# The reciprocals of the key features' sums: one VectorE instruction per batch becomes four GpSimd instructions

## The chip, the cores and the metric

The kernel runs on one core of a Trainium2 chip. The time is device microseconds of one execution of the whole program. "Before" is the median of three runs, and a further execution was profiled. TensorE multiplies matrices into the PSUM memory, VectorE (DVE in the rows) and ScalarE (ACT) compute on SBUF and PSUM, GpSimd (POOL) computes on SBUF alone, and SyncE (SP) issues DMAs. Each engine runs its own list of instructions in order and waits on semaphores that the others raise.

## The reference, cut to what matters

There are 32 batches of 256 tokens with 128 channels, in 16 heads of 8. Each batch is normalised and projected to q, k and v. The output mixes a sparse attention (the 12 largest scores of each row) with a linear one, on softmax features of q and k:

```python
q = _layernorm(q, q_gamma, q_beta)
k = _layernorm(k, k_gamma, k_beta)
scores = jnp.einsum('bhnd,bhmd->bhnm', q, k) / jnp.sqrt(jnp.float32(D))
aw = jax.nn.softmax(scores, axis=-1)
kth = jax.lax.top_k(aw, topk)[0][..., -1:]
...
kf = jax.nn.softmax(k, axis=-1)
kv = jnp.einsum('bhnd,bhne->bhde', kf, v)
```

The change concerns `kf`: the exponentials of a key's 8 values are divided by their sum. With 256 tokens on 128 partitions and 16 heads, that makes 32 sums on each partition and batch.

## The kernel before, in words

Every engine walks the same loop: iterations `it` from -2 to 33, and in each eight units `u_` of two heads. A unit holds four score tiles of 128x256. Iteration `it` works on batch `it`'s scores and prepares batch `it + 1`; its last units serve the batches on both sides. The order on each engine is the written order of its block.

One unit passes through the engines like this:

- TensorE makes the scores (L907). VectorE takes the 8 largest of each row from the four tiles (`largest`, `top`, L613).
- GpSimd subtracts the maximum (`drop`, L402), and ScalarE makes the exponentials of the four tiles (`e`, L803) and of the 8 largest (`e8`, L808).
- One unit later VectorE removes the 8 largest from `e` (`remove`, L620, which waits for `e8`) and takes the next 8 (`following`, `next8`, L626). Between these stand small steps for the other stages (`extra`).
- One more unit later GpSimd and ScalarE share the comparisons (`below`). GpSimd makes `POOL_TILES` = 3, 2, 3, 4, 4, 4, 3, 2 of the four tiles for the eight units (L424), in its own units 2 to 7, 0 and 1. TensorE then transposes, and so on.

On GpSimd, `drop` of a unit stands ahead of the unit's other work, and so behind all of the unit before it.

The key features of batch `it + 1`: ScalarE makes `k_exp` (L844); GpSimd adds the 8 values in three steps in unit 5 (`k_half`, `k_quarter`, `k_sum`, L453); VectorE takes the reciprocal in unit 6 (`k_rec`, L685), ahead of its last `following`; GpSimd multiplies in unit 7 (`k_feat`, L460).

Ahead of batch 0 stands a prologue. There VectorE passes the reciprocal of batch 0 in iteration -1, and then runs `stage_gate` (L585 to L602), which chooses one of eight feed-forward matrices, ahead of its first `top`.

Of the kernel before, what the change touches and what calls it, by code (L numbers as in the profile page):

```python
# [26 lines left out]
ALU = mybir.AluOpType  # L27
# [3 lines left out]
P = 128  # L31
H = 16
# [3 lines left out]
NT = N // P  # L36
# [48 lines left out]
def build(nc, x, Wqkv, bqkv, q_gamma, q_beta, k_gamma, k_beta, alpha, Wproj, bproj, W, bW, logits, u, y):  # L85
# [12 lines left out]
    def exists(batch):  # L98
        return not isinstance(batch, int) or 0 <= batch < B

    with ExitStack() as ctx:
        def sb(name, shape, dt=F32):
            return ctx.enter_context(nc.sbuf_tensor(name, shape, dt))
# [4 lines left out]
        def sem(name):  # L108
            return ctx.enter_context(nc.semaphore(name))
# [60 lines left out]
        k_half = sb("k_half", [P, NT * H, 4])  # L170
        k_quarter = sb("k_quarter", [P, NT * H, 2])
        k_sum = sb("k_sum", [P, NT * H])
        k_rec = sb("k_rec", [P, NT * H])
        k_feat = sb("k_feat", [P, NT, C])
        v_aug = sb("v_aug", [P, 2, NT, H, VW])
# [34 lines left out]
            x_stats x_mean x_rsqrt_step x_rsqrt_ready x_newton xn_ready  # L210
            w_xT xT_copied w_qk_ready sq_ready sq_step raw_ready ss_ready qk_rsqrt_step qk_rsqrt_ready qk_newton
            n_step qkn_ready w_qkT w_rest part_ready slots_written first_loaded slots_loaded
            dmax_ready dsub_ready dexp_ready ksum_step ksum_ready krec_ready feat_ready
            w_v_ready v_copied w_kv kv_ready w_qfT qfT_copied w_lin linz_step lin_ready
            w_turn den_step osp_ready w_osT osT_copied w_out y_ready""".split()
        s = {n: sem(n) for n in names}
# [68 lines left out]
        def _(pool):  # L285
            def select(out, op, fill, base_, pattern, mult, n):
                pool.wait_ge(s["pool_step"], n)
                return nc.gpsimd.affine_select(out=out, in_=out, compare_op=op, fill=fill, base=base_,
                                               pattern=pattern, channel_multiplier=mult)
# [11 lines left out]
            for par in range(2):  # L301
                nc.gpsimd.memset(v_aug[:, par, :, :, D:VA], 1.0).then_inc(s["pool_const"], 1)
            nc.gpsimd.memset(top[:], 0.0).then_inc(s["pool_const"], 1)
            nc.gpsimd.memset(eps_row[:], 0.0).then_inc(s["pool_step"], 1)
            pool.wait_ge(s["pool_step"], 6)
            nc.gpsimd.memset(eps_row[:, :, D:VA], Z_EPS).then_inc(s["pool_const"], 1)
# [5 lines left out]
            select(used, ALU.not_equal, 1.0, 0, [[-VW, 4], [-1, VA]], 1, 7).then_inc(s["gather_ready"], 1)  # L312
            select(spare, ALU.not_equal, 1.0, -VA, [[-VW, 4], [-1, VW - VA]], 1, 7).then_inc(s["gather_ready"], 1)
            select(minus_one[:], ALU.not_equal, -1.0, 0, [[-1, P]], 1, 8).then_inc(s["gather_ready"], 1)
            pool.wait_ge(s["pool_const"], 7)
            gb = gamma[:].rearrange("p a h d -> p (a h d)")
            bb = beta[:].rearrange("p a h d -> p (a h d)")

# [72 lines left out]
            def body(it, par, xr):  # L391
                nxt = 1 - par
                for u_ in range(UNITS):
                    if (it, u_) == (-2, 7):
                        stage_shares()
                    g = it * UNITS + u_
                    if exists(it):

                        q = u_ % 2
                        wait(pool, s["e8_ready"], g - 1)  # L400
                        wait_alone(pool, s["top_ready"], TILES * (g + 1), s["waits_passed"])
                        nc.gpsimd.tensor_tensor(drop[:, q], top[:, q], top[:, q, :, 1:2].to_broadcast(  # L402
                            [P, TILES, 9]), ALU.subtract).then_inc(s["drop_ready"], 1)
                    if u_ == 0 and it >= 0 and exists(it + 1):

                        pool.wait_ge(s["sq_ready"], it + 2)
                        src = qk_sq[:].rearrange("p (g d) -> p g d", d=D)
                        for i, (dst, w) in enumerate(((sq_half[:], 4), (sq_quarter[:], 2),
                                                      (qk_ss[:].unsqueeze(2), 1))):
                            if i:  # L410
                                pool.wait_ge(s["sq_step"], 2 * it + i)
                            nc.gpsimd.tensor_tensor(dst, src[:, :, 0:w], src[:, :, w:2 * w], ALU.add).then_inc(
                                s["sq_step" if i < 2 else "ss_ready"], 1)
                            src = dst
                    if u_ == 2 and it >= 0 and exists(it + 1):
                        normalise(it, 1)
                    if u_ == 3 and it >= 0 and exists(it + 1):
                        normalise(it, 2)
                    if exists(it if u_ >= 2 else it - 1):

                        r = (u_ - 2) % RING
                        for t in range(POOL_TILES[r]):
                            wait_alone(pool, s["next_ready"], TILES * (g - 2) + t + 1, s["waits_passed"])
                            nc.gpsimd.tensor_scalar(below[:, r, t, :], e[:, r, t, :],  # L424
                                                    next8[:, r, t, TOPK - 9:TOPK - 8], None,
                                                    ALU.is_lt).then_inc(s["below_pool"], 1)
                    if u_ == 1 and it >= 0 and exists(it + 1):
                        normalise(it, 0)
                    if u_ == 3 and it >= 0 and exists(it + 1):

                        pool.wait_ge(s["dmax_ready"], it + 2)
                        nc.gpsimd.tensor_tensor(heads(d_sub[:]), heads(qkn[:]), spread(d_max[:]),
                                                ALU.subtract).then_inc(s["dsub_ready"], 1)
                    if u_ == 4 and it >= -1 and exists(it + 2):

                        pool.wait_ge(s["x_rsqrt_ready"], 2 * (it + 3))
                        n = X_STEPS * (it + 2)
                        refine(x_rsqrt, "x", n)
                        pool.wait_ge(s["x_newton"], n + 3)
                        nc.gpsimd.tensor_tensor(x_shift[:, 0], x_mv[:, :, 0], x_rsqrt[:, 3],  # L440
                                                ALU.mult).then_inc(s["x_newton"], 1)
                        wait_alone(pool, s["x_newton"], n + 4, s["waits_passed"])
                        nc.gpsimd.tensor_scalar(x_shift[:, 1], x_shift[:, 0], -1.0, None,
                                                ALU.mult).then_inc(s["x_newton"], 1)
                    if u_ == 5 and exists(it + 1):

                        pool.wait_ge(s["dexp_ready"], 2 * (it + 2))
                        src = k_exp[:].rearrange("p t (h d) -> p (t h) d", d=D)
                        for i, (dst, w) in enumerate(((k_half[:], 4), (k_quarter[:], 2),
                                                      (k_sum[:].unsqueeze(2), 1))):  # L450
                            if i:
                                pool.wait_ge(s["ksum_step"], 2 * (it + 1) + i)
                            nc.gpsimd.tensor_tensor(dst, src[:, :, 0:w], src[:, :, w:2 * w], ALU.add).then_inc(  # L453
                                s["ksum_step" if i < 2 else "ksum_ready"], 1)
                            src = dst
                    if u_ == 7 and exists(it + 1):

                        pool.wait_ge(s["krec_ready"], it + 2)
                        pool.wait_ge(s["dexp_ready"], 2 * (it + 2))
                        nc.gpsimd.tensor_tensor(k_feat[:].rearrange("p t (h d) -> p (t h) d", d=D),  # L460
                                                k_exp[:].rearrange("p t (h d) -> p (t h) d", d=D),
                                                k_rec[:].unsqueeze(2).to_broadcast([P, NT * H, D]),
                                                ALU.mult).then_inc(s["feat_ready"], 1)
# [4 lines left out]
        def _(dve):  # L468
# [73 lines left out]
            def stage_normalise():  # L542
# [34 lines left out]

                dve.wait_ge(s["bq_centred"], 1)
                in_parts(b_row[:, 0:2 * C], slice(0, 2 * C)).then_inc(s["bqk_ready"], 1)
                dve.wait_ge(s["pool_const"], 7)  # L580
                nc.vector.tensor_tensor(own_head[:, :, 0:D], own_head[:, :, 0:D],
                                        mix[:, 6, :].unsqueeze(2).to_broadcast([P, H, D]),
                                        ALU.mult).then_inc(s["head_ready"], 1)
# [23 lines left out]
            def body(it, par, xr):  # L607
# [20 lines left out]
                def extra(u_, k):  # L628
# [25 lines left out]
                    if u_ == 5 and 1 <= k <= 4 and exists(it - 1):  # L654
                        w = pv_ps[:, 0:NT * H * VA].rearrange("p (g e) -> p g e", e=VA)
                        n = 2 * (it - 1)
# [14 lines left out]
                    if u_ == 1 and exists(it + 2):  # L671
# [5 lines left out]
                        if k == 5:  # L677
# [2 lines left out]
                            alone(s["x_newton"], X_STEPS * (it + 2))  # L680
                            for t in range(NT):
                                nc.vector.bn_aggr(x_mv[:, t], stats[:, t]).then_inc(s["x_mean"], 1)  # L682
                    if u_ == 6 and exists(it + 1) and k == 5:
                        dve.wait_ge(s["ksum_ready"], it + 2)
                        nc.vector.reciprocal(k_rec[:], k_sum[:]).then_inc(s["krec_ready"], 1)  # L685

                for u_ in range(UNITS):
                    if (it, u_) == (-2, 2):
# [192 lines left out]
        def _(pe):  # L881
# [8 lines left out]
            def body(it, par, xr):  # L890
# [76 lines left out]
                def early(u_):  # L967
# [47 lines left out]
                    if u_ == 7 and exists(it + 2):  # L1015

                        pe.wait_ge(s["xT_copied"], it + 4)
                        if it == -2:
                            pe.wait_ge(s["wqk_ready"], 1)
                            pe.wait_ge(s["bq_centred"], 1)  # L1020
                            pe.wait_ge(s["pool_const"], 7)
                            pe.wait_ge(s["gather_ready"], 4)
                        if it == -1:
                            pe.wait_ge(s["bqk_ready"], 1)
# [93 lines left out]
```

## Time and profile before

| | |
|---|---|
| median of 3 runs (lowest to highest) | 1223.74 us (1223.39 to 1226.09) |
| the profiled execution | 1223.17 us |
| its span, first to last instruction | 1221.4 us |
| mean granted TensorE clock | 0.978 of full speed |
| VectorE busy | 1186.8 us, 97% of the span |
| ScalarE busy | 1086.6 us, 89% |
| GpSimd busy | 1081.7 us, 89% |
| TensorE busy | 959.2 us, 79% |

The 1.8 us between the profiled execution and its span lie outside of the first and the last instruction. Shares of busy time are averages over the span; idle time counts only where it delays the engine that ends last.

### The profile page before, as it was taken

To read this page: it belongs to the slowest core of one execution; us is meant where nothing else is said; L and a number is where in the kernel's file an instruction comes from. 1 tells how busy PE (TensorE), PEld (TensorE's weight loads), DVE (VectorE), ACT (ScalarE), POOL (GpSimd) and SP (SyncE) were. 2 spreads that over 40 slices of the span, in tenths; PEclk is the share of its full clock that TensorE was granted. 3 is DMA by queue.
4 is the path that set the end of the run, shared out by engine and by line. 5 is a ranking of instruction groups with operands and counts; after the bars stand their busy time and mean duration, and the time that the engine had idled before them with its cause. 6 is when DMAs were issued, how large, how long until landed. Compare 5 with 4: busy or idle time off the path is not lost.

```text
span 1221.4 us, 34664 instructions
## 1 busy us (share of the span) xinstructions
PE 959.2 (79%) x8999; PEld 651.6 (53%) x9030; DVE 1186.8 (97%) x4540; ACT 1086.6 (89%) x3626; POOL 1081.7 (89%) x1688
## 2 busy tenths in 40 slices
PE   4478878788887887887888877878787878887776
PEld 2255555555555555555555555555555555555554
DVE  5999999999999999999999999999999999999994
ACT  3589999999999999899999999999999999999984
POOL 5599999999999999999999999999999999999964
PEclk9999999999999999999989999999999999999998
DMA  3122221222221212221112222122222122222110
GB/s 94 30 62 79 84 83 40 69 60 83 84 83 50 62 57 84 84 84 55 56 58 84 83 84 60 55 67 70 84 83 80 40 62 70 83 84 79 45 45 14
DMA packets 165127, 82.78 MB, mean 68 GB/s; under 512 B 7737, under 2 KB 164927, under 8 KB 164930
## 3 DMA queue, kind: packets, MB, share of 16 engines
q1 hardware_dynamic: 164658, 80.43, 22.9%
q8 instruction: 74, 1.21, 0.4%
q14 instruction: 123, 1.01, 0.3%
q10 hardware_dynamic: 272, 0.13, 0.0%
HBM read 42.78 MB, written 37.75 MB: 66 GB/s over the span
## 4 chain that ended last, share of the span: by engine, by line
DVE 64%; issue 25%; DVEq 4%; PE 4%; ACT 2%; POOL 1%; DMA 0%; POOLq 0%; ACTq 0%
DVE rest L620 27%; DVE top L613 22%; DVE next L626 9%; DVEq L75 4%; DVE o_sparse L668 1%; DVE lin_z L641 1%; POOL below L424 1%; ACT e L803 1%; PE turn_ps L925 1%; DVE stats L676 0%; DVE den L660 0%; DVE kv L634 0%; PE work_ps L1027 0%; DVE x_mv L682 0%; PE pv_ps L946 0%
## 5 line engine op out<-in xcount | busy, mean ns | idle before, releaser
L424 POOL TENSOR_SCALAR below<-e,next 128x256 bf16<-128x256 f32 x800 | 724.3, 921 | 0.7 <-issue 0.6
L803 ACT ACTIVATE e<-score_ps,drop 128x256 f32<-128x256 f32 x1024 | 471.6, 478 | 67.5 <-POOL drop L402 63.9
L620 DVE MATCH_REPLACE8 rest<-e 128x256 f32<-128x256 f32 x1024 | 432.7, 431 | 0.0
L925 PE MATMUL turn_ps<-ident,e 128*128 128x128 f32 x2048 | 397.5, 288 | 39.6 <-ACT kept L773 18.3
L626 DVE MAX8 next<-rest 128x8 f32<-128x256 f32 x1024 | 427.7, 434 | 0.3 <-issue 0.2
L926 PE MATMUL turn_ps<-minus_huge,below 128*128 128x128 bf16 x2048 | 377.0, 224 | 0.0
L613 DVE MAX8 top<-score_ps 128x8 f32<-128x256 f32 x1024 | 365.5, 436 | 1.1 <-PE score_ps L907 1.1
L925 PEld LDWEIGHTS turn_ps<-ident,e 128*128 128x128 f32 x2048 | 295.5, 144 | 76.7 <-issue 32.5
L773 ACT ACTIVATE kept<-turn_ps 128x1024 f32<-128x1024 f32 x256 | 267.5, 1045 | 32.8 <-PE turn_ps L926 32.4
L926 PEld LDWEIGHTS turn_ps<-minus_huge,below 128*128 128x128 bf16 x2048 | 221.2, 108 | 0.7
L803 ACT ACTIVATION_READ_ACCUMULATOR e<-score_ps,drop 128x1 f32 x1024 | 214.9, 210 | 0.0
L946 PE MATMUL pv_ps<-kept,v_aug 128*32 128x256 f32 x2048 | 142.8, 398 | 1.9 <-ACT out_sb L849 1.3
L402 POOL TENSOR_TENSOR drop<-top 128x36 f32<-128x36 f32 x256 | 62.7, 245 | 64.4 <-DVE top L613 63.9
L907 PE MATMUL score_ps<-k_slots,q_slots 64*128 64x256 bf16 x1024 | 102.8, 278 | 20.8 <-issue 9.9
L816 ACT ACTIVATE below<-e,next 128x256 bf16<-128x256 f32 x224 | 107.7, 514 | 0.0
L620 DVE MATCH_VALUE_LOAD rest<-e 128x8 f32 x1024 | 97.7, 95 | 1.9 <-ACT e L808 1.9
L946 PEld LDWEIGHTS pv_ps<-kept,v_aug 128*32 128x32 f32 x2048 | 55.3, 112 | 48.8 <-issue 28.8
L907 PEld LDWEIGHTS score_ps<-k_slots,q_slots 64*128 64x128 bf16 x1024 | 30.7, 94 | 79.8 <-issue 72.4
L1027 PE MATMUL work_ps<-w_qk,xnT 128*128 128x256 f32 x128 | 46.8, 449 | 31.1 <-ACT xnT L865 31.1
L808 ACT ACTIVATE e<-drop 128x32 f32<-128x32 f32 x256 | 62.7, 245 | 0.0
L957 PE MATMUL pv_ps<-gather,oT 128*128 128x128 f32 x256 | 35.0, 280 | 33.1 <-ACT oT L825 33.1
L1049 PE MATMUL work_ps<-kv,qfT 128*128 128x144 f32 x128 | 25.1, 321 | 40.3 <-DVE kv L634 40.3
(182 smaller groups left out, 1341.1 us busy)
## 6 DMA issues: line engine op xcount, KB each, us to landing
part_slots<-part SPq DMA_DIRECT2D x128, 192.0 KB, 2.3
q_slots<-part_slots SPq DMA_DIRECT2D x64, 256.0 KB, 3.4
k_slots<-part_slots SPq DMA_DIRECT2D x64, 256.0 KB, 4.1
part_slots<-part SPq DMA_DIRECT2D x64, 128.0 KB, 1.9
x_sb<-in_L_attn_x SPq DMA_DIRECT2D x32, 128.0 KB, 4.0
x_res<-in_L_attn_x SPq DMA_DIRECT2D x32, 128.0 KB, 3.9
out_y<-out_sb SPq DMA_DIRECT2D x32, 128.0 KB, 4.1
w_ops<-in_L_ffn_W SPq DMA_DIRECT2D x1, 512.0 KB
```

The costliest lines, as they stand in the source:

```text
L402: nc.gpsimd.tensor_tensor(drop[:, q], top[:, q], top[:, q, :, 1:2].to_broadcast([P, TILES, 9]), ALU.subtract).then_inc(s["drop_ready"], 1)
L424: nc.gpsimd.tensor_scalar(below[:, r, t, :], e[:, r, t, :], next8[:, r, t, TOPK - 9:TOPK - 8], None, ALU.is_lt).then_inc(s["below_pool"], 1)
L613: nc.vector.max(top[:, q, t, 1:9], score_ps[:, q, t // 2, t % 2, :]).then_inc(s["top_ready"], 1)
L620: nc.vector.match_replace(rest[:, t, :], e8[:, (u_ - 1) % 2, t, :], e[:, (u_ - 1) % RING, t, :], REMOVED).then_inc(s["rest_ready"], 1)
L626: nc.vector.max(next8[:, (u_ - 1) % RING, t, :], rest[:, t, :]).then_inc(s["next_ready"], 1)
L773: nc.scalar.activation(kept[:, u_ % 4], turn_ps[:], ACT.Relu).then_inc(s["turn_copied"], 1)
L803: nc.scalar.activation(e[:, u_ % RING, t, :], score_ps[:, u_ % 2, t // 2, t % 2, :], ACT.Exp, bias=drop[:, u_ % 2, t, 0:1], accum_out=z[:, ...
L816: nc.scalar.activation(below[:, r, t, :], e[:, r, t, :], ACT.Relu, scale=-1.0, bias=next8[:, r, t, TOPK - 9:TOPK - 8]).then_inc(s["below_a ...
L907: last = mm(score_ps[:, v_ % 2, hh, nt, :], q_slots[rows, side, v_, nt * P:(nt + 1) * P], k_slots[rows, side, v_, :], start=True, stop=True)
L925: mm(dst, e[:, r, t, keys], ident[:], start=True, stop=False, is_transpose=True)
L926: last = mm(dst, below[:, r, t, keys], minus_huge[:], start=False, stop=True)
L946: last = mm(pv_ps[32 * j:32 * (j + 1), 0:N], v_aug[:, side, mc, 4 * q + j, :], kept[:, v_ % 4, j % 2, mc, :], start=(mc == 0), stop=(mc == ...
```

## The change

VectorE's reciprocal goes. GpSimd makes `k_rec` in unit 6, behind its comparisons of that unit: a power (`k_sum` to the -1, with the exponents read from a tile `inverse` that is filled once), and a Newton step on it in three instructions, each of which waits for the one before. The four stand ahead of unit 7's `drop`.

```diff
+        inverse = sb("inverse", [P, NT * H])
+        k_power = sb("k_power", [P, 2, NT * H])
...
+            nc.gpsimd.memset(inverse[:], -1.0).then_inc(s["pool_const"], 1)
...
-            pool.wait_ge(s["pool_const"], 7)
+            pool.wait_ge(s["pool_const"], 8)
...
+                    if u_ == 6 and exists(it + 1):
+
+                        first, near = k_power[:, 0], k_power[:, 1]
+                        n = 3 * (it + 1)
+                        pool.wait_ge(s["ksum_ready"], it + 2)
+                        nc.gpsimd.tensor_tensor(first, k_sum[:], inverse[:], ALU.pow).then_inc(s["krec_step"], 1)
+                        pool.wait_ge(s["krec_step"], n + 1)
+                        nc.gpsimd.tensor_tensor(near, first, k_sum[:], ALU.mult).then_inc(s["krec_step"], 1)
+                        pool.wait_ge(s["krec_step"], n + 2)
+                        nc.gpsimd.tensor_scalar(near, near, -1.0, 2.0, ALU.mult, ALU.add).then_inc(s["krec_step"], 1)
+                        pool.wait_ge(s["krec_step"], n + 3)
+                        nc.gpsimd.tensor_tensor(k_rec[:], first, near, ALU.mult).then_inc(s["krec_ready"], 1)
...
-                    if u_ == 6 and exists(it + 1) and k == 5:
-                        dve.wait_ge(s["ksum_ready"], it + 2)
-                        nc.vector.reciprocal(k_rec[:], k_sum[:]).then_inc(s["krec_ready"], 1)
```

VectorE's and TensorE's waits for `pool_const` go from 7 to 8 in the same way.

On GpSimd, units 5 to 7 of iteration 0 (preparing batch 1) read as follows before:

```order
L453 TENSOR_TENSOR k_sum<-k_quarter 128x32 [waits ksum_step]
L402 TENSOR_TENSOR drop<-top 128x36 [waits top_ready,e8_ready]
L424 TENSOR_SCALAR below<-e,next 128x256 [waits next_ready] x4
L402 TENSOR_TENSOR drop<-top 128x36 [waits top_ready,e8_ready]
L424 TENSOR_SCALAR below<-e,next 128x256 [waits next_ready] x4
L460 TENSOR_TENSOR k_feat<-k_exp,k_rec 128x256 [waits dexp_ready,krec_ready]
```

And with the change, from unit 6 on:

```order
L405 TENSOR_TENSOR drop<-top 128x36 [waits top_ready,e8_ready]
L427 TENSOR_SCALAR below<-e,next 128x256 [waits next_ready] x4
L464 TENSOR_TENSOR k_power<-k_sum,inverse 128x32 [waits ksum_ready]
L466 TENSOR_TENSOR k_power<-k_power,k_sum 128x32 [waits krec_step]
L468 TENSOR_SCALAR k_power<-k_power 128x32 [waits krec_step]
L470 TENSOR_TENSOR k_rec<-k_power 128x32 [waits krec_step]
L405 TENSOR_TENSOR drop<-top 128x36 [waits top_ready,e8_ready]
L427 TENSOR_SCALAR below<-e,next 128x256 [waits next_ready] x4
L475 TENSOR_TENSOR k_feat<-k_exp,k_rec 128x256 [waits dexp_ready,krec_ready]
```

The four new rows stand between unit 6's comparisons and unit 7's `drop`; nothing else moved there. The line numbers of the same instructions grow by 3 to 15.

In the prologue VectorE's rows around the reciprocal of batch 0 are these before (`bias` and `own_head` are the last steps of the stage ahead, the `gate` rows are the start of `stage_gate`):

```order
L489 SCALAR_TENSOR_TENSOR bias<-bias_rest,ident,bias_sum 3x256 [waits setup_p]
L581 TENSOR_TENSOR own_head<-own_head,mix 128x16x8 [waits pool_const]
L685 RECIPROCAL k_rec<-k_sum 128x32 [waits ksum_ready]
L587 TENSOR_SCALAR gate<-gate 128x8 [waits gate_logs]
L588 TENSOR_TENSOR gate<-gate 128x8 [waits setup_p]
```

And with the change:

```order
L504 SCALAR_TENSOR_TENSOR bias<-bias_rest,ident,bias_sum 3x256 [waits setup_p]
L596 TENSOR_TENSOR own_head<-own_head,mix 128x16x8 [waits pool_const]
L602 TENSOR_SCALAR gate<-gate 128x8 [waits gate_logs]
L603 TENSOR_TENSOR gate<-gate 128x8 [waits setup_p]
L604 TENSOR_REDUCE gate<-gate 128x1 [waits setup_p]
```

The reciprocal is gone, and with it VectorE's wait for `ksum_ready`: `stage_gate` follows at once.

## Rows read from the trace of the kernel before

**Rows 1.** The page's first part: busy us (share of the span) and instructions.

```profile
PE 959.2 (79%) x8999; PEld 651.6 (53%) x9030; DVE 1186.8 (97%) x4540; ACT 1086.6 (89%) x3626; POOL 1081.7 (89%) x1688
```

**Rows 2.** The chain that ended last, shares of the span by engine.

```profile
DVE 64%; issue 25%; DVEq 4%; PE 4%; ACT 2%; POOL 1%; DMA 0%; POOLq 0%; ACTq 0%
```

**Rows 3.** VectorE's timeline in a middle batch: start, duration in us.

```profile
647.18 1.42 DVE L613 MAX8 top<-score_ps 128x8 f32<-128x256 f32 x4
...
651.05 0.34 DVE L685 RECIPROCAL k_rec<-k_sum 128x32 f32<-128x32 f32 x1
...
651.59 1.41 DVE L613 MAX8 top<-score_ps 128x8 f32<-128x256 f32 x4
...
655.79 1.42 DVE L613 MAX8 top<-score_ps 128x8 f32<-128x256 f32 x4
657.12 0.08 DVE L620 MATCH_VALUE_LOAD rest<-e 128x8 f32 x1
...
666.04 0.08 DVE L620 MATCH_VALUE_LOAD rest<-e 128x8 f32 x1
```

**Rows 4.** Groups of VectorE's instructions: busy us, mean ns, idle before.

```profile
L685 DVE RECIPROCAL k_rec<-k_sum 128x32 f32<-128x32 f32 x32 | 11.4, 356 | 1.8 <-POOL k_sum L453 1.8
...
L660 DVE SCALAR_TENSOR_TENSOR den<-z,pv_ps 128x32 f32<-128x32 f32 x32 | 6.4, 200 | 11.2 <-PE pv_ps L957 11.2
```

**Rows 5.** VectorE's timeline in the prologue.

```profile
23.82 0.27 DVE L581 TENSOR_TENSOR own_head<-own_head,mix 128x128 f32<-128x128 f32 x1
25.89 0.35 DVE L685 RECIPROCAL k_rec<-k_sum 128x32 f32<-128x32 f32 x1 [1.80 <-POOL k_sum L453]
26.16 0.13 DVE L587 TENSOR_SCALAR gate<-gate 128x8 f32<-128x8 f32 x1
...
36.65 2.73 DVE L613 MAX8 top<-score_ps 128x8 f32<-128x256 f32 x8
```

**Rows 6.** TensorE's timeline in the prologue: the second unit's scores.

```profile
32.57 0.61 PE L907 MATMUL score_ps<-k_slots,q_slots 64*128 64x256 bf16 x4
```

**Rows 7.** GpSimd's timeline in the prologue: the first `drop`.

```profile
38.23 0.25 POOL L402 TENSOR_TENSOR drop<-top 128x36 f32<-128x36 f32 x1 [11.28 <-DVE top L613]
```

**Rows 8.** GpSimd's timeline in the middle batch; idle time before, and its releaser.

```profile
639.75 0.25 POOL L402 TENSOR_TENSOR drop<-top 128x36 f32<-128x36 f32 x1 [0.70 <-DVE top L613]
...
648.54 0.29 POOL L453 TENSOR_TENSOR k_quarter<-k_half 128x64 f32<-128x64 f32 x1
648.91 0.24 POOL L453 TENSOR_TENSOR k_sum<-k_quarter 128x32 f32<-128x32 f32 x1
...
653.21 0.24 POOL L402 TENSOR_TENSOR drop<-top 128x36 f32<-128x36 f32 x1 [0.27 <-DVE top L613]
...
670.77 0.24 POOL L402 TENSOR_TENSOR drop<-top 128x36 f32<-128x36 f32 x1 [0.26 <-DVE top L613]
...
674.32 1.08 POOL L432 TENSOR_TENSOR d_sub<-qkn,d_max 128x512 f32<-128x512 f32 x1 [0.28 <-DVE d_max L652]
```

**Rows 9.** GpSimd's waits over the span: us in total, times, longest.

```profile
POOL drop L402 <- DVE top L613: 63.9, 104, 11.3
POOL d_sub L432 <- DVE d_max L652: 8.3, 29, 0.3
```

**Rows 10.** Groups of GpSimd's instructions: busy us, mean ns, idle before.

```profile
L350 POOL TENSOR_TENSOR qk_b<-qk_a,gamma 128x512 f32<-128x512 f32 x31 | 39.5, 1273 | 0.0
...
L453 POOL TENSOR_TENSOR k_sum<-k_quarter 128x32 f32<-128x32 f32 x32 | 7.6, 238 | 2.5
...
L333 POOL TENSOR_SCALAR qk_rsqrt<-qk_rsqrt 128x64 f32<-128x64 f32 x31 | 7.5, 243 | 6.2 <-POOL qk_rsqrt L331 6.2
```

**Rows 11.** ScalarE's timeline in the middle batch.

```profile
653.49 0.47 ACT L803 ACTIVATE e<-score_ps,drop 128x256 f32<-128x256 f32 x1 [0.60 <-POOL drop L402]
...
655.30 0.24 ACT L808 ACTIVATE e<-drop 128x32 f32<-128x32 f32 x1
...
664.48 0.23 ACT L808 ACTIVATE e<-drop 128x32 f32<-128x32 f32 x1
```

More of the change, by code:

```diff
@@ L212, in build @@
             n_step qkn_ready w_qkT w_rest part_ready slots_written first_loaded slots_loaded
-            dmax_ready dsub_ready dexp_ready ksum_step ksum_ready krec_ready feat_ready
+            dmax_ready dsub_ready dexp_ready ksum_step ksum_ready krec_step krec_ready feat_ready
             w_v_ready v_copied w_kv kv_ready w_qfT qfT_copied w_lin linz_step lin_ready
@@ L579, in stage_normalise @@
                 in_parts(b_row[:, 0:2 * C], slice(0, 2 * C)).then_inc(s["bqk_ready"], 1)
-                dve.wait_ge(s["pool_const"], 7)
+                dve.wait_ge(s["pool_const"], 8)
                 nc.vector.tensor_tensor(own_head[:, :, 0:D], own_head[:, :, 0:D],
@@ L1020, in early @@
                             pe.wait_ge(s["bq_centred"], 1)
-                            pe.wait_ge(s["pool_const"], 7)
+                            pe.wait_ge(s["pool_const"], 8)
                             pe.wait_ge(s["gather_ready"], 4)
```

## The prediction, made before the changed kernel ran

> **What bounds the kernel now.** I read the busy times first: VectorE is busy for 1186.8 of 1221.4 us, the others for 89% or less [rows 1]. The chain that ended last says the same: 64% of it is VectorE's work and 25% "issue", time in which nothing that the profile shows was waited for [rows 2]. VectorE's timeline in a middle batch has no marked wait: from one `top` to the next a unit takes 4.41 us where the reciprocal stands in it (647.18 to 651.59) and 4.20 us in the next one (to 655.79) [rows 3]. So in the steady part every step that leaves VectorE's list shortens the batch, as long as no other engine becomes the bound.
>
> The next question is how far GpSimd is from that, since it takes the work. Its waits for VectorE in one batch are 0.27, 0.26 and 0.70 us ahead of three `drop`s and 0.28 us ahead of `d_sub` [rows 8]: **1.51 us** of real room a batch. Over the span it is (63.9 - 11.3 + 8.3) / 31 = 1.96 us a batch, with the prologue's one long wait taken out [rows 9]. That mean holds batches in which VectorE was itself held up, so I go by 1.51. GpSimd is thus nearly a second bound.
>
> **What is removed.** VectorE runs 32 reciprocals, 31 of them in the steady part and one in the prologue. Their profiled duration is 356 ns [rows 4], but instructions overlap on that engine, and what counts is the longer unit: 4.41 - 4.20 = 0.21 us [rows 3]. 31 x 0.21 = **6.5 us**. The upper bound is the full duration, 31 x 0.356 = 11.0 us; the difference of the units is the nearer reading, as it holds the overlap.
>
> The one in the prologue is worth more. `own_head` begins at 23.82 and ends at 24.09; VectorE then waits 1.80 us for `k_sum`, and `stage_gate` begins only at 26.16 [rows 5]. Without the reciprocal it begins at about 24.1: **2.07 us** earlier. Everything from there to the first `top` at 36.65 is VectorE's own work in a row, and the first two units' scores have been ready since 33.18 [rows 6], ahead of the new 34.6. So the whole steady part starts 2.07 us earlier. This gain doesn't hang on GpSimd's price: behind the first `k_feat` GpSimd waits 11.28 us for that `top` [rows 7], and even when 2.07 us of it go, four dearer steps fit. The one `memset` of `inverse` lies in the setup, beside other engines' loads, and is put at nothing; uncovered it would be one small instruction, once.
>
> **What is added.** Four dependent steps on GpSimd a batch, behind unit 6's comparisons and ahead of unit 7's `drop`. The trace has prices for three: a two-input step on 128x32 takes 238 ns, a scalar step on 128x64 243 ns (an upper bound for 128x32) [rows 10]. A dependent step starts 0.08 us behind the end of the one before: 648.54 + 0.29 to 648.91 [rows 8]. So the Newton step and its gaps are 3 x 0.24 + 3 x 0.08 = 0.96 us.
>
> **The power** is in no row. From below: it reads two 128x32 tensors and writes one, as the add that makes `k_sum` does, and can hardly be cheaper: 0.24 us. From above, the dearest repeated step of this engine of the same kind, 128x512 with sixteen times the elements, takes 1.27 us [rows 10]; a power at that price costs sixteen adds an element. I take 0.24 us, by the row that has its shape and engine, and keep 1.27 for the range. The sum is then 0.96 + 0.24 = **1.20 us a batch**.
>
> The Trainium skill speaks against moving such work: by its page "GPSIMD Engine Reference" (section 4.1, Engine selection) GpSimd is about twice as slow as VectorE at two-input elementwise steps. Here VectorE takes 200 ns for a two-input step on 128x32 and GpSimd 238 [rows 4, 10], a factor of 1.2, so the trace doesn't agree at this size; rival C says what the factor would cost.
>
> **Where the 1.20 us go.** What stands behind them on GpSimd is `drop` of unit 7, and ScalarE waits for it: 0.60 us already now [rows 11]. That `drop` has 0.27 us of idle time ahead of it [rows 8], so it comes 1.20 - 0.27 = 0.93 us later. ScalarE's `e8` of that unit ends at 655.54 [rows 11], and VectorE asks for it at 657.12 [rows 3]: 1.58 us of room, 1.37 with VectorE 0.21 ahead. Two units on, `e8` ends at 664.71 and is asked for at 666.04 [rows 3, 11]: 1.33 us, 1.12 then. 0.93 fits in both, with 0.19 to spare at the tighter one. GpSimd makes the time up again in units 3 and 4, where its other waits are.
>
> Over a whole batch: GpSimd's room of 1.51 falls by the 0.21 that VectorE saves, to 1.30; 1.20 of it are used. VectorE stays the bound with 0.10 us left on GpSimd. So the power may cost 0.24 + 0.10 = **0.34 us** for free; what it costs above that comes back 31 times:
>
> time = 1223.17 - 2.07 - 6.5 + 31 x (power - 0.34 us, if that is positive).
>
> **The sum** for a power of 0.24 us: 1223.17 - 8.6 = **1214.6 us**. It is made against the profiled execution, which is 0.57 us below the median of 1223.74.
>
> **The rivals.** A measurement of this kernel can tell about 0.2% from no change, 2.45 us: faster is below 1221.3, slower above 1226.2.
>
> *A. The power is dear, and GpSimd becomes the bound.* It would show as full idle-free GpSimd and VectorE waiting for ScalarE's `e8`, since `drop` comes late. It decides from a power of 0.34 + (1226.2 - 1214.6) / 31 = 0.71 us on, three times the add. For it speaks that a power is more than one arithmetic step an element, and that GpSimd has 1.51 us in all; against it only that no row prices such a step. At the bound of 1.27 us: 1214.6 + 31 x 0.93 = 1243.4 us. Chance 0.38.
>
> By the Trainium skill's "GPSIMD Engine Reference" (section 7, Performance pitfalls for Q7 kernels) a dependent fp32 chain costs 4 cycles an element on that engine, whose clock the page gives as 1.2 GHz. 
>
> *C. Every one of the four steps costs twice what VectorE takes*, the rule of "GPSIMD Engine Reference" above. Worked from rows, 2 x 0.20 = 0.40 us each, with gaps 4 x 0.40 + 0.24 = 1.84 us, 0.54 over the room of 1.30: 1214.6 + 31 x 0.54 = 1231.3 us, slower. The rows of 238 and 243 ns speak against it [rows 10]. Chance 0.03.
>
> **How the numbers follow.** The forecast, a power near the price of an add, has 0.47: it is the likeliest, though not more likely than all others together. Faster 0.47, within 0.2% 0.12, slower 0.38 + 0.03 = 0.41. The forecast's own range is 1212.5 (some of the reciprocal's duration beyond 0.21 us is freed too) to 1219 (the power at 0.48 us). For the range of 8 in 10 the top is rival A at its bound, 1243.4; dearer powers, some 0.17, stay outside, and 0.03 below 1212.5.
>
> **What would show it right or wrong.** In the changed profile: L685's wait and step gone from the prologue, first `top` near 34.6 us; units 6 and 7 on VectorE alike at 4.20 us; the power's own duration in GpSimd's groups, which decides nearly all; GpSimd's waits for `top` down to about 0.1 us a batch; no waits of VectorE for `e8`. The forecast is wrong if the power takes over 0.34 us. In that case GpSimd has no waits left, ScalarE waits for `drop` in every unit, and VectorE's waits for `e8` carry 31 times the excess.

## The result, and the profile after

The changed kernel takes **1382.45 us** (median of 4 runs, 1379.87 to 1384.31) beside 1223.57 us for the kernel before (4 runs). The ratio is 1.1299, with a 95% interval of [1.1275, 1.1324]: 13% slower. Ratios below are followed by their interval in the same way. The forecast was 1214.6 us in a range of 1212.5 to 1243.4.

The page of the changed kernel's profiled execution (1381.92 us), first part and then the chain that ended last, answers to [rows 1, 2]:

```profile
PE 1033.5 (75%) x9030; PEld 686.4 (50%) x9030; DVE 1190.1 (86%) x4508; ACT 1084.2 (79%) x3626; POOL 1277.1 (93%) x1817
...
POOL 40%; DVE 27%; issue 20%; ACT 6%; PE 5%; DVEq 1%; POOLq 1%; DMA 0%; ACTq 0%
POOL below L427 19%; POOL k_power L464 12%; DVE rest L635 11%; DVE top L628 9%; ACT e L815 4%; DVE next L641 3%; DVEq L75 1%; POOL drop L405 1%; PE turn_ps L937 1%; POOL qkn L353 1%; POOL k_half L456 1%; POOL d_sub L435 1%; POOL k_power L466 1%; POOLq L75 1%; PE turn_ps L938 1%
```

GpSimd has taken VectorE's place: 40% of the chain, and its busy time is 195.4 us longer. Its groups (busy us, mean ns, idle before) say on what, beside [rows 10]:

```profile
L464 POOL TENSOR_TENSOR k_power<-k_sum,inverse 128x32 f32<-128x32 f32 x32 | 174.8, 5461 | 0.1
L405 POOL TENSOR_TENSOR drop<-top 128x36 f32<-128x36 f32 x256 | 63.0, 246 | 28.7 <-DVE top L628 28.4 <-issue 0.2
...
L466 POOL TENSOR_TENSOR k_power<-k_power,k_sum 128x32 f32<-128x32 f32 x32 | 8.0, 252 | 2.5
L470 POOL TENSOR_TENSOR k_rec<-k_power 128x32 f32<-128x32 f32 x32 | 8.0, 251 | 2.7
...
L468 POOL TENSOR_SCALAR k_power<-k_power 128x32 f32<-128x32 f32 x32 | 7.0, 218 | 3.0
```

**The power takes 5461 ns**, 23 times the add of the same shape. The Newton step's three instructions cost what was foreseen. GpSimd's timeline in a middle batch, beside [rows 8]:

```profile
646.77 0.25 POOL L405 TENSOR_TENSOR drop<-top 128x36 f32<-128x36 f32 x1 [0.91 <-DVE top L628]
647.00 3.61 POOL L427 TENSOR_SCALAR below<-e,next 128x256 bf16<-128x256 f32 x4
650.58 5.46 POOL L464 TENSOR_TENSOR k_power<-k_sum,inverse 128x32 f32<-128x32 f32 x1
656.12 0.25 POOL L466 TENSOR_TENSOR k_power<-k_power,k_sum 128x32 f32<-128x32 f32 x1
656.46 0.22 POOL L468 TENSOR_SCALAR k_power<-k_power 128x32 f32<-128x32 f32 x1
656.76 0.25 POOL L470 TENSOR_TENSOR k_rec<-k_power 128x32 f32<-128x32 f32 x1
656.97 0.25 POOL L405 TENSOR_TENSOR drop<-top 128x36 f32<-128x36 f32 x1
```

From 650.58 to 656.97 unit 7's `drop` stands behind the chain. ScalarE's timeline has the wait for it, and VectorE's the wait for ScalarE's `e8` in the unit after, beside [rows 11] and [rows 3]:

```profile
657.25 0.47 ACT L815 ACTIVATE e<-score_ps,drop 128x256 f32<-128x256 f32 x1 [6.24 <-POOL drop L405]
```

```profile
653.57 1.42 DVE L628 MAX8 top<-score_ps 128x8 f32<-128x256 f32 x4
...
659.47 0.09 DVE L635 MATCH_VALUE_LOAD rest<-e 128x8 f32 x1 [4.49 <-ACT e L820]
...
662.37 1.41 DVE L628 MAX8 top<-score_ps 128x8 f32<-128x256 f32 x4
```

That unit lasts 8.80 us (653.57 to 662.37) and lasted 4.20. Over the span the waits are:

```profile
ACT e L815 <- POOL drop L405: 235.9, 84, 7.0
...
PE work_ps L988 <- ACT qk_raw L883: 159.9, 31, 6.1
DVE rest L635 <- ACT e L820: 151.6, 39, 5.1
```

The chain drop, exponentials, removal is the one that rival A named, at a price far beyond its bound. Two of its signs came weaker than foreseen: GpSimd still waits 28.4 us for `top`, and ScalarE waits for `drop` 84 times, not in every one of the 256 units. In the prologue, VectorE's first `top` and GpSimd's first `drop`, beside [rows 5, 7]:

```profile
34.81 2.73 DVE L628 MAX8 top<-score_ps 128x8 f32<-128x256 f32 x8
```

```profile
36.40 0.25 POOL L405 TENSOR_TENSOR drop<-top 128x36 f32<-128x36 f32 x1 [2.34 <-DVE top L628]
```

`top` begins 1.84 us earlier (36.65 before), and even the dear power fits ahead of the first `drop`, with 2.34 us left.

### The profile page after: what moved, and what is told of

It is laid out like the page before. It is cut to its first block, busy times and chain, and to the rows that moved or that the text cites. A ratio compares the mean times of both kernels' runs of the same rounds, so it can differ in the third digit from the quotient of the medians.

```text
span 1380.2 us, 34792 instructions
## 1 busy us (share of the span) xinstructions
PE 1033.5 (75%) x9030; PEld 686.4 (50%) x9030; DVE 1190.1 (86%) x4508; ACT 1084.2 (79%) x3626; POOL 1277.1 (93%) x1817
## 4 chain that ended last, share of the span: by engine, by line
POOL 40%; DVE 27%; issue 20%; ACT 6%; PE 5%; DVEq 1%; POOLq 1%; DMA 0%; ACTq 0%
POOL below L427 19%; POOL k_power L464 12%; DVE rest L635 11%; DVE top L628 9%; ACT e L815 4%; DVE next L641 3%; DVEq L75 1%; POOL drop L405 1%; PE turn_ps L937 1%; POOL qkn L353 1%; POOL k_half L456 1%; POOL d_sub L435 1%; POOL k_power L466 1%; POOLq L75 1%; PE turn_ps L938 1%
## 5 line engine op out<-in xcount | busy, mean ns | idle before, releaser
L937 PE MATMUL turn_ps<-ident,e 128*128 128x128 f32 x2048 | 435.3, 305 | 20.3 <-ACT kept L785 13.9
L635 DVE MATCH_REPLACE8 rest<-e 128x256 f32<-128x256 f32 x1024 | 418.3, 413 | 0.0
L641 DVE MAX8 next<-rest 128x8 f32<-128x256 f32 x1024 | 410.9, 418 | 0.2 <-issue 0.2
L938 PE MATMUL turn_ps<-minus_huge,below 128*128 128x128 bf16 x2048 | 409.6, 235 | 0.0
L937 PEld LDWEIGHTS turn_ps<-ident,e 128*128 128x128 f32 x2048 | 316.4, 154 | 93.8 <-issue 39.1
L938 PEld LDWEIGHTS turn_ps<-minus_huge,below 128*128 128x128 bf16 x2048 | 233.3, 114 | 0.8 <-issue 0.2
L635 DVE MATCH_VALUE_LOAD rest<-e 128x8 f32 x1024 | 81.2, 79 | 156.3 <-ACT e L820 151.6
L464 POOL TENSOR_TENSOR k_power<-k_sum,inverse 128x32 f32<-128x32 f32 x32 | 174.8, 5461 | 0.1
L988 PE MATMUL work_ps<-ident,q_exp 128*128 128x128 f32 x64 | 21.1, 433 | 159.9 <-ACT qk_raw L883 159.9
L919 PE MATMUL score_ps<-k_slots,q_slots 64*128 64x256 bf16 x1024 | 113.9, 303 | 21.2 <-issue 9.0
L405 POOL TENSOR_TENSOR drop<-top 128x36 f32<-128x36 f32 x256 | 63.0, 246 | 28.7 <-DVE top L628 28.4
```

The costliest lines, as they stand in the source:

```text
L464: nc.gpsimd.tensor_tensor(first, k_sum[:], inverse[:], ALU.pow).then_inc(s["krec_step"], 1)
L635: nc.vector.match_replace(rest[:, t, :], e8[:, (u_ - 1) % 2, t, :], e[:, (u_ - 1) % RING, t, :], REMOVED).then_inc(s["rest_ready"], 1)
L641: nc.vector.max(next8[:, (u_ - 1) % RING, t, :], rest[:, t, :]).then_inc(s["next_ready"], 1)
L919: last = mm(score_ps[:, v_ % 2, hh, nt, :], q_slots[rows, side, v_, nt * P:(nt + 1) * P], k_slots[rows, side, v_, :], start=True, stop=True)
L937: mm(dst, e[:, r, t, keys], ident[:], start=True, stop=False, is_transpose=True)
L938: last = mm(dst, below[:, r, t, keys], minus_huge[:], start=False, stop=True)
```

## The experiments

Each was run beside the kernel before on the same chip; that kernel's medians were 1222.64, 1222.86 and 1221.89 us for the three groups of runs.

**1. The power replaced by a multiplication.**

```diff
-                        nc.gpsimd.tensor_tensor(first, k_sum[:], inverse[:], ALU.pow).then_inc(s["krec_step"], 1)
+                        nc.gpsimd.tensor_tensor(first, k_sum[:], inverse[:], ALU.mult).then_inc(s["krec_step"], 1)
```

> The changed kernel with the power replaced by a multiplication of the same two 128x32 tensors into the same tile; its result is not a reciprocal, so the key features are left wrong, and everything else stands. Theory P (the power's 5.46 us on GpSimd make the loss, all else is as the forecast had it): the step takes 0.24 us, GpSimd's list fits again, and the time is 1214.6 us, between 1212.5 and 1219. Rival R (the chain itself costs: four dependent steps and their waits ahead of unit 7's drop): the time stays above 1230 us.

Measured: 1222.37 us beside 1222.64, ratio 1.000 [0.999, 1.001]. The loss of 13% is gone, so theory P holds for it: it is the power's price. But the gain of 8.6 us isn't there either. Neither number was met, and a second question opens: where did VectorE's saving go? It isn't the price of the steps, which take 1.19 us up to `drop`, as summed:

```profile
468.54 0.26 POOL L464 TENSOR_TENSOR k_power<-k_sum,inverse 128x32 f32<-128x32 f32 x1
...
469.73 0.25 POOL L405 TENSOR_TENSOR drop<-top 128x36 f32<-128x36 f32 x1
```

VectorE's unit 6 is short, as foreseen (4.20 us from `top` to `top`), and the quickest batches last 36.14 us, 0.2 less than the usual 36.34 before. But 11 of 28 batches (2 to 29) last more than 36.5 us, and 3 of 28 did before (both counted from VectorE's `top` of a batch's first unit to the next batch's). In one of them TensorE's timeline reads (`oT` is ScalarE's copy of one of TensorE's results):

```profile
842.52 0.30 PE L997 MATMUL pv_ps<-ident,o_sparse 128*128 128x128 f32 x1 [1.62 <-ACT oT L837]
...
844.98 0.48 PE L937 MATMUL turn_ps<-ident,e 128*128 128x128 f32 x1
...
849.60 0.61 PE L919 MATMUL score_ps<-k_slots,q_slots 64*128 64x256 bf16 x4
```

and VectorE's, in which it now waits for scores in unit 3:

```profile
850.39 0.76 DVE L628 MAX8 top<-score_ps 128x8 f32<-128x256 f32 x2 [0.52 <-PE score_ps L919]
```

The stretch of 8 us around it has a granted clock of 0.62 (PEclk, in shares of full speed; ahead of it the busy us of PE, PEld, DVE, ACT and POOL, behind it the DMA share and GB/s):

```profile
842.00:850.00 8.00, 7.48 (x50) 4.34 (x50) 7.88 (x34) 7.37 (x26) 7.64 (x13) 0.62 0.01 2
```

In a batch of the kernel before, TensorE waits for `oT` just as long, and 8 us behind that wait have 1.00:

```profile
660.73 0.30 PE L985 MATMUL pv_ps<-ident,o_sparse 128*128 128x128 f32 x1 [1.61 <-ACT oT L825]
```

```profile
661.36:669.36 8.00, 6.43 (x67) 4.50 (x66) 8.00 (x35) 7.77 (x31) 7.64 (x12) 1.00 0.02 4
```

So in run 1 TensorE ran part of the 8 us at 1.2 GHz instead of 2.4, after a wait for ScalarE of 1.62 us, and its scores came late. From 200 to 1100 us the clock is 0.95 here and 0.98 in the kernel before.

A lower clock by itself need not lengthen a batch. These are the whole batch of run 1 around the rows above, and one of the kernel before with the same clock:

```profile
836.44:873.50 37.06, 32.44 (x293) 22.06 (x292) 36.37 (x141) 33.95 (x116) 34.84 (x57) 0.91 0.23 66
```

```profile
619.46:655.80 36.34, 31.79 (x287) 21.46 (x290) 36.34 (x142) 33.69 (x114) 33.60 (x53) 0.91 0.23 67
```

Of the 28 batches of each profiled execution, run 1 has eight with a mean clock of 0.91 and the later run 6, which has the same four steps, three: all eleven last over 36.5 us. The kernel before and runs 4, 5, 8 and 10 have eleven together, of which nine last 36.15 to 36.41 us and two 37.63 and 37.89.

**2. The power over half of the columns.**

```diff
-                        nc.gpsimd.tensor_tensor(first, k_sum[:], inverse[:], ALU.pow).then_inc(s["krec_step"], 1)
+                        nc.gpsimd.tensor_tensor(first[:, 0:H], k_sum[:, 0:H], inverse[:, 0:H], ALU.pow).then_inc(s["krec_step"], 1)
```

> The changed kernel with the power over 16 of the 32 columns; the others keep a constant, so half of the heads' key features are wrong. It asks what the 5.46 us are made of. If they go by the element, with the 0.17 us that remain of the add's 238 ns when its 32 elements are taken off at the rate of the 128x512 row, the power takes 0.17 + 5.29 / 2 = 2.82 us, and theory P gives 1214.6 + 31 x (2.82 - 0.34) = 1291.5 us, up to 1300 with the 8.6 us that the same sum misses for the changed kernel (1373.3 against 1381.9). If they are a fixed price of the instruction, 1382 us. Rival R: 1382 us, as the chain is the same.

Measured: 1306.54 us, ratio 1.0683 [1.0667, 1.0699]. The power's row (min, median, max ns):

```profile
L465 POOL TENSOR_TENSOR k_power<-k_sum,inverse x32: 2935/2940/2945, 26.9 to 1242.2; 128x16 f32<-128x16 f32 x32
```

Sixteen columns less save 2521 ns: the power costs 158 ns an element and 0.42 us beside. It goes by the element, against the rival of a fixed price. The price is 0.12 us above the 2.82 of the expectation, and the time lies above its 1300. The time follows the price in a straight line from run 1: 1222.4 + 31 x (2.94 - 0.26) = 1305.5, and 1222.4 + 31 x (5.46 - 0.26) = 1383.6 (0.26 is the multiplication's own row), beside 1306.5 and 1382.5 measured.

**3. The chain moved behind unit 7's drop.**

```diff
-                    if u_ == 6 and exists(it + 1):
+                    if u_ == 7 and exists(it + 1):
```

(the block stands right behind `drop`, ahead of the comparisons)

> The changed kernel with the four steps moved behind unit 7's drop, ahead of unit 7's comparisons. Theory P: GpSimd's list is as full as before, so the stall moves from VectorE's unit 0 to its unit 1 and the time stays between 1373 and 1385 us. The rival that blames the place (unit 7's drop is held up by the chain): with that drop free the time falls most of the way, to 1250 us or less.

Measured: 1404.44 us, ratio 1.1485 [1.1468, 1.1502]: 22 us more than the changed kernel. The place ahead of `drop` is not to blame. Theory P's "between 1373 and 1385" is missed too: unit 7's comparisons now stand behind the power, and TensorE waits for them, beside ScalarE and VectorE, whose waits are about as long as in the changed kernel (that this makes the 22 us is read from the waits, not tested):

```profile
ACT e L815 <- POOL drop L405: 228.0, 83, 6.9
...
PE turn_ps L937 <- POOL below L439: 182.2, 61, 6.0
DVE rest L635 <- ACT e L820: 161.1, 44, 5.4
```

**4. The prologue's term alone.** In the kernel before, VectorE takes batch 0's reciprocal behind `stage_gate`.

```diff
                         stage_gate()
+                        dve.wait_ge(s["ksum_ready"], 1)
+                        nc.vector.reciprocal(k_rec[:], k_sum[:]).then_inc(s["krec_ready"], 1)
...
-                    if u_ == 6 and exists(it + 1) and k == 5:
+                    if u_ == 6 and it >= 0 and exists(it + 1) and k == 5:
```

> The kernel before with one edit: in the prologue VectorE takes batch 0's reciprocal behind stage_gate and not ahead of it; the 31 others stay. It tests the prologue's term alone. If that term is real, the first top comes near 34.8 us as in the changed kernel and the time falls by 1.8 us, to 1221.8. The rival: the lead is lost again to another wait, and the time stays at 1223.6 us.

Measured: 1220.61 us beside 1222.64, ratio 0.998 [0.9969, 0.999]: 2.0 us. Its first `top` begins at 34.32 us. The term is real, and no later wait takes it back.

**5. The removal alone.** VectorE's reciprocal goes, nothing comes to GpSimd.

```diff
-            nc.gpsimd.memset(inverse[:], -1.0).then_inc(s["pool_const"], 1)
+            nc.gpsimd.memset(k_rec[:], 0.25).then_inc(s["pool_const"], 1)
...
-                    if u_ == 6 and exists(it + 1):
...
-                        pool.wait_ge(s["krec_ready"], it + 2)
```

> The removal alone: VectorE's reciprocal goes, GpSimd gets nothing in its place, and k_rec is a constant, so the key features are left unnormalised and wrong. The first multiplication run came out at 1222.4 us beside 1222.6 for the kernel before, where the forecast's sum gave 1214. Theory T (the removal is worth its 2.0 + 6.5 us, and the 1.2 us a batch of cheap steps on GpSimd ate it): 1214.1 us, up to 1216. Rival V (the 0.21 us a batch that VectorE saves are worth nothing, since another engine is late next): the prologue's 2.0 us alone, 1220.6 us.

Measured: 1215.28 us beside 1222.86, ratio 0.9933 [0.9912, 0.9955]: 7.6 us, theory T. VectorE's 0.21 us a batch are worth what the sum gave them, as far as the interval (5.5 to 10.8 us in all) tells. The usual batch of the profiled execution (the median of the 28) lasts 36.15 us beside 36.34. TensorE's clock from 200 to 1100 us is 0.98.

**6. The addition alone, cheap.** The chain as four multiplications into a spare tile; VectorE keeps its reciprocal.

```diff
+                        nc.gpsimd.tensor_tensor(first, k_sum[:], inverse[:], ALU.mult).then_inc(s["krec_step"], 1)
...
+                        nc.gpsimd.tensor_tensor(k_spare[:], first, near, ALU.mult).then_inc(s["krec_step"], 1)
```

> The addition alone at a low price: VectorE keeps its reciprocal and its place, and GpSimd runs the four steps as multiplications into a tile that nobody reads. The output is the reference's. By the forecast's arithmetic 1.20 us fit in GpSimd's room of 1.51 us and the time stays at 1222.6 us. Theory T (these steps make drop late, TensorE idles and falls to its lower clock in some batches): what the multiplication run lost comes back here, 1222.6 + 8 = 1229 to 1231 us. Rival V (the steps cost nothing): 1222.6 us.

Measured: 1226.26 us beside 1222.86, ratio 1.0031 [1.0017, 1.0044]: 3.4 us slower by the medians. Neither number is met. The steps do cost, though they fit by their sum, and they cost about half of the 7 us that they cost with the reciprocal gone (1222.37 against 1215.28), where the room is 0.21 us smaller.

**7. The addition alone, dear.** As 6, with the power.

> The addition alone at the dear price: the four steps with the power, into a tile that nobody reads, and VectorE's reciprocal kept. Theory P: VectorE isn't the bound any more, so its reciprocal costs nothing in the steady part, and only the prologue's 2 us come back: 1384 us. The rival, that where k_rec is made matters (a later k_rec holds up the products on TensorE): clearly below the changed kernel, 1370 us or less.

Measured: 1383.23 us, ratio 1.1314 [1.1292, 1.1336]. Adding a power that nobody reads makes the whole loss. VectorE's reciprocals are all there and cost nothing that shows in the steady part, as theory P has it: the time lies 0.8 us above the changed kernel's, where the prologue alone was put at 2.

**8. One multiplication in the chain's place.**

```diff
+                        pool.wait_ge(s["ksum_ready"], it + 2)
+                        nc.gpsimd.tensor_tensor(k_rec[:], k_sum[:], inverse[:], ALU.mult).then_inc(s["krec_ready"], 1)
```

> VectorE's reciprocal gone and one multiplication on GpSimd in its place, at the chain's place, instead of four steps (the key features are left wrong). It adds about 0.26 us a batch to GpSimd, far inside its room. Theory G: 1215 us, as with nothing in the reciprocal's place, up to 1217. The rival, that any step ahead of unit 7's drop costs: a quarter of the four steps' 7 us or more, 1217 to 1222 us.

Measured: 1215.63 us beside 1221.89, ratio 0.9945 [0.9932, 0.9959]. Theory G's number is met: a single step in that place costs far less than the four. Whether it costs nothing isn't settled, since the ratio lies 0.0012 (1.5 us) above run 5's, within the intervals, and the rival's quarter of 7 us is 1.75.

**9. Four multiplications, and room for them.** As run 1, with one comparison tile a batch moved to ScalarE.

```diff
-POOL_TILES = (3, 2, 3, 4, 4, 4, 3, 2)
+POOL_TILES = (3, 2, 3, 4, 4, 3, 3, 2)
```

> The run with four multiplications and VectorE's reciprocal gone (key features wrong, as there), and one of the 25 comparison tiles of a batch moved from GpSimd to ScalarE: the sixth entry of POOL_TILES goes from 4 to 3, so GpSimd's unit 7, right behind the chain, has three. It gives GpSimd 0.92 us a batch back and ScalarE 0.5 us more. Theory G (cheap steps cost 7 us because GpSimd has no room left, so that late drops and comparisons reach TensorE): with room the whole gain comes, 1215 us, up to 1217. The rival (the chain's dependent waits or ScalarE's load cost, whatever the room): 1221 us or more.

Measured: 1212.74 us beside 1221.89, ratio 0.9922 [0.9908, 0.9937]. With room on GpSimd the same four steps cost nothing that shows. GpSimd's idle time ahead of `drop` shows the room, run 1 first, then this one:

```profile
L405 POOL TENSOR_TENSOR drop<-top 128x36 f32<-128x36 f32 x256 | 63.8, 249 | 33.4 <-DVE top L628 32.3 <-issue 0.2
```

```profile
L405 POOL TENSOR_TENSOR drop<-top 128x36 f32<-128x36 f32 x256 | 62.7, 245 | 49.0 <-DVE top L628 47.0 <-issue 0.2
```

What the moved tile does for the kernel by itself wasn't tried. The traces narrow it down: the usual batch lasts 36.15 us here as in runs 5 and 8, where no tile was moved, so the tile doesn't shorten it. What differs from run 1 is the number of batches over 36.5 us, 4 of 28 and not 11.

**10. The reciprocal on ScalarE.** Nothing stands in its place on VectorE or GpSimd, and `k_rec` is the same quantity as before.

```diff
+                    if u_ == 6 and exists(it + 1):
+                        act.wait_ge(s["ksum_ready"], it + 2)
+                        nc.scalar.activation(k_ln[:], k_sum[:], ACT.Ln).then_inc(s["krec_step"], 1)
+                        act.wait_ge(s["krec_step"], it + 2)
+                        nc.scalar.activation(k_rec[:], k_ln[:], ACT.Exp, scale=-1.0).then_inc(s["krec_ready"], 1)
...
-                        nc.vector.reciprocal(k_rec[:], k_sum[:]).then_inc(s["krec_ready"], 1)
```

> Another home for the reciprocal: ScalarE takes the logarithm of the sums and the exponential of its negative, two steps on 128x32 in unit 6, behind the copy of xnT and ahead of the next copy of kept; VectorE and GpSimd get nothing in its place. Theory T: VectorE saves 2.0 + 6.5 us, ScalarE's 0.5 us lie in the 0.6 us for which it waits for unit 7's drop: 1214.1 us, up to 1217. Rival V: 1220.6 us, the prologue alone, or more if the two steps delay kept and with it TensorE.

Measured: **1214.50 us** beside 1222.86, ratio 0.9928 [0.9911, 0.9946]. This version is 0.7% faster than the kernel before and beats the changed one too. ScalarE's timeline in unit 6 and 7:

```profile
644.37 0.40 ACT L863 COPY xnT<-work_ps 128x256 f32<-128x256 f32 x1
644.63 0.27 ACT L866 ACTIVATE k_ln<-k_sum 128x32 f32<-128x32 f32 x1
644.93 0.23 ACT L868 ACTIVATE k_rec<-k_ln 128x32 f32<-128x32 f32 x1
645.07 1.01 ACT L771 ACTIVATE kept<-turn_ps 128x1024 f32<-128x1024 f32 x1
646.06 0.47 ACT L801 ACTIVATE e<-score_ps,drop 128x256 f32<-128x256 f32 x1
```

The two steps delay `kept` by 0.44 us (644.63 to 645.07), and `e` of unit 7, which waited 0.60 us for `drop` [rows 11], follows with no wait.

## Why the prediction was wrong

**The step that failed is the power's price**: "I take 0.24 us, by the row that has its shape and engine, and keep 1.27 for the range". It measured 5.46 us. The lower bound was the add of the same shape, the upper one an arithmetic step over sixteen times the elements; both are adds and multiplications, and neither says anything of a power. The range's top was set by a row that bounds another operation. 31 x (5.46 - 0.24) = 162 us is nearly the whole miss of 168 us, and run 7 shows it by itself. The prediction left a chance of 0.17 for a power dearer than that bound.

Beside the forecast stood the Trainium skill's "GPSIMD Engine Reference" (section 7, Performance pitfalls for Q7 kernels) with 4 cycles an element for a dependent fp32 step at 1.2 GHz. By that figure, as an estimate, the 158 ns an element of run 2 are as long as 47 such steps in a row; the 20 that I had assumed are fewer than half of them. That the power is such a chain is not shown.

A smaller reading was loose: the 200 ns of VectorE's two-input step belong to a step that reads one operand from PSUM (`den<-z,pv_ps`), and GpSimd's 238 ns to one on SBUF alone, so the factor of 1.2 doesn't compare like with like. Rival C is out by the Newton steps' own rows, 0.25, 0.22 and 0.25 us and not 0.40.

**The second step that failed is "VectorE stays the bound with 0.10 us left on GpSimd".** Run 1 has the price that I had assumed and comes out at 1222.4 us, not 1214.6. This is rival B's second half: a sum over one middle batch said that 1.20 us fit in 1.30. In an undisturbed batch they do (36.14 us, the whole saving), but 11 of 28 batches are disturbed and lose more than it. Runs 8 and 9 point to the missing room: with one step in place of four, or with a tile less on GpSimd, the gain is there, 6.3 and 9.2 us beside run 5's 7.6. That the long batches come by way of TensorE's lower clock is read from run 1's rows. It isn't separated from other ways in which a late `drop` might hurt, and the kernel before has a wait of the same length at the same place (TensorE for `oT`) without the fall, so what tips the clock stays open. The batches with a clock of 0.91 say that the fall does harm mostly where the four steps stand. Run 6 costs only half as much as run 1 says; its trace has three such batches and run 1's eight, and the mean clock of its 12 runs is 0.965 (0.966 before), that of run 1's 12 runs 0.954 (0.969 before). So a rarer fall is a likely reason, not a shown one.

**What held.** The prologue: 2.07 us foreseen, 2.0 measured in run 4, with 1.84 us of `top`'s start in the changed kernel. The steady gain: 6.5 us foreseen; run 5 has 7.6 in all, run 4 has 2.0 of them, so 5.6 remain, within what such runs tell apart. The Newton step took 0.93 us from the power's end to `drop` (656.04 to 656.97), beside 0.96 foreseen. The way of the stall (`drop`, `e8`, VectorE's removal) is that of rival A, and VectorE's waits for `e8` come to 151.6 us beside 31 x (5.46 - 0.34) = 158.7. The line's slope of 31 us a microsecond holds from 0.26 to 5.46 us of price. Its zero doesn't: at 5.46 us the forecast's own line gives 1373.3, 9 us below the measured time, about as much as the 8 us that run 1 misses.

## What to carry to other kernels

An operation that no row of the trace shows has no upper bound in the rows of other operations: measure it by itself, or put nothing on a full engine on the strength of it. An engine whose work fits in a batch by its sum with a tenth of a microsecond to spare is already the bound, since disturbed batches don't recover. By the same sums 0.3 us of room (run 6: 1.51 less 1.20) still cost 3.4 us, and about 1.0 us (run 8: 1.30 less the one step's 0.26; run 9: 0.10 and the tile's 0.92) cost nothing that shows. Look for the engine that waits next to the step that moves: ScalarE waited 0.60 us at that very place, and there the reciprocal was nearly free.

## What the runs showed of the hardware that was not expected

- GpSimd's power of two fp32 tensors takes 2.94 us for 128x16 and 5.46 us for 128x32: 0.42 us and 158 ns an element, where the rows of a multiplication and an add give 2.2 ns an element, (1273 - 238) / 480 [rows 10].
- ScalarE makes the same reciprocals, as a logarithm and an exponential, in 0.27 + 0.23 us.
- One TensorE wait of 1.6 us is followed by a stretch of lower granted clock in some batches and not in others: 0.62 over 8 us in the batch shown from run 1, 1.00 in the batch of the kernel before.
- A batch with a mean granted clock of 0.91 is long where GpSimd has 0.1 to 0.3 us of room (11 of 11 in runs 1 and 6) and mostly not where it has about 1.0 us or more (2 of 11 in the kernel before and runs 4, 5, 8 and 10). This is read from one profiled execution of each.
